# Moving the copy of the transposed V from ScalarE to VectorE in the attention stage of a transformer layer

## The reference, cut to what matters

```python
# layer: x = x + attn(layernorm(x)); x = x + ffn(layernorm(x))   x: 1 x 8192 x 2048, fp32
def attn(x, w_qkv, w_proj):                 # 16 heads of 128
    qkv = (x @ w_qkv.T).reshape(B, N, 3, H, hd)
    q, k, v = (qkv[:, :, 0], qkv[:, :, 1], qkv[:, :, 2])
    att = jnp.einsum('bnid,bnjd->bnij', q, k) * hd ** (-0.5)   # over the 16 heads of one row
    att = jax.nn.softmax(att, axis=-1)
    out = jnp.einsum('bnij,bnjd->bnid', att, v)
    out = out.transpose(0, 2, 1, 3).reshape(B, N, D)
    return out @ w_proj.T
def ffn(x, kernel, bias):                   # 8-bit fake quantisation of x, kernel, bias, y
    y = jax.nn.relu(fq(x, -1) @ fq(kernel, 0) + fq(bias, -1))
    return fq(y, -1)
```

## Time and profile before

| | us |
|---|---|
| Time, median of 2 runs | 911.78 (911.33 to 912.23) |
| The profiled execution: its own time | 915.79 |
| its span, slowest core (core 6) | 914.2 |
| spans of the 8 cores | 902.3 to 914.2 |
| VectorE busy | 553.4 (61%) |
| ScalarE busy | 336.6 (37%) |
| TensorE matmuls busy | 692.9 (76%) |

### The profile page before, as it was taken

One profiled execution on the slowest core, in us unless ns is written; L12 is line 12 of the kernel. 1 busy time (PEld: TensorE's weight loads), 2 busy tenths in 40 slices (PEclk: granted clock), 3 DMA queues, 4 the chain that ended last, 5 costly groups with the idle time before them and its releaser, 6 DMA issues.

```text
span 914.2 us, 11027 instructions; the slowest of 8 cores (902.3 to 914.2 us)
## 1 busy us (share of the span) xinstructions
PE 692.9 (76%) x3584; PEld 339.7 (37%) x3584; DVE 553.4 (61%) x917; ACT 336.6 (37%) x395; POOL 110.9 (12%) x93
## 2 busy tenths in 40 slices
PE   1158999899999999994555568974985756978891
PEld 1023444344444444443444434530332323433340
DVE  3352335345554554434555528993598896899997
ACT  3366334233433433435666622220121334333320
POOL 1000111111111111100000000002000000123214
PEclk9998999899999999996555568985798967999996
DMA  9462999899999999857522354459322200111112
GB/s 165 137 187 16 83 77 149 121 145 148 162 146 147 157 156 103 77 47 200 133 35 36 38 160 138 130 125 184 83 80 92 93 0 1 47 47 47 63 75 92
DMA packets 116983, 94.19 MB, mean 103 GB/s; under 512 B 101184, under 2 KB 101312, under 8 KB 113856
## 3 DMA queue, kind: packets, MB, share of 16 engines
q0 software_dynamic: 103680, 33.56, 38.5%
q1 hardware_dynamic: 13248, 59.94, 19.2%
HBM read 118.65 MB, written 8.39 MB: 139 GB/s over the span
## 4 chain that ended last, share of the span: by engine, by line
DVE 19%; PE 17%; issue 8%; DMA 5%; ACT 4%; DVEq 1%; POOLq 0%; POOL 0%; ACTq 0%; SPq 0%
DMA wpb<-wpT 4%; PE pF L535 3%; PE pF L499 3%; PE pF L502 3%; DVE bnbuf L588 2%; PE pF L343 2%; PE pH L334 2%; ACT aTTbuf L368 2%; ACT V8buf L362 2%; DVE ttile L796 2%; DVE cols L653 2%; PE pF L324 1%; PE pH L317 1%; DVE cols L799 1%; DVE ktb L685 1%
## 5 line engine op out<-in xcount | busy, mean ns | idle before, releaser
L286 PE MATMUL pF<-aT,wqb 128*128 128x512 bf16 x736 | 280.7, 381 | 5.8 <-DMA wqb<-wqkvT 5.8
L288 PE MATMUL pF<-aT,wqb 128*128 128x512 bf16 x736 | 280.5, 381 | 0.0
L499 PE MATMUL pF<-wpb,sT 128*128 128x512 bf16 x256 | 105.7, 413 | 24.2 <-DMA wpb<-wpT 22.1
L535 PE MATMUL pF<-qk,xqs 128*128 128x512 bf16 x512 | 118.8, 395 | 3.7 <-ACT xqs L882 3.7
L286 PEld LDWEIGHTS pF<-aT,wqb 128*128 128x128 bf16 x736 | 72.4, 98 | 95.1 <-issue 9.5
L502 PE MATMUL pF<-wpb,sT 128*128 128x512 bf16 x256 | 106.0, 414 | 0.0
L288 PEld LDWEIGHTS pF<-aT,wqb 128*128 128x128 bf16 x736 | 72.3, 98 | 87.3 <-issue 1.7
L301 POOL DMA_DIRECT2D wqb<-wqkvT x48 | 55.0, 1146 | 339.7 <-PE pF L288 250.9
L113 DVE CAST qT<-pF 128x512 bf16<-128x512 f32 x16 | 42.7, 2671 | 73.9 <-PE pF L288 59.3
L113 DVE CAST vT<-pF 128x512 bf16<-128x512 f32 x16 | 42.8, 2673 | 58.7 <-PE pF L288 58.7
L535 PEld LDWEIGHTS pF<-qk,xqs 128*128 128x128 bf16 x512 | 51.6, 102 | 67.7 <-issue 13.0
(11 more groups left out here) (116 smaller groups left out, 855.6 us busy)
## 6 DMA issues: line engine op xcount, KB each, us to landing
wqb<-wqkvT POOLq DMA_DIRECT2D x48, 512.0 KB, 10.0
ktc<-wkT SPq DMA_DIRECT2D x32, 512.0 KB, 8.3
ktb<-wkT SPq DMA_DIRECT2D x32, 512.0 KB, 3.8
xbuf<-x_att SPq DMA_DIRECT2D x8, 1024.0 KB, 6.3
xr<-x_res SPq DMA_DIRECT2D x8, 1024.0 KB, 7.5
wpb<-wpT POOLq DMA_DIRECT2D x32, 256.0 KB, 5.9
out<-xr SPq DMA_DIRECT2D x7, 1024.0 KB, 3.8
bias_b<-bias SPq DMA_DIRECT2D x1, 1024.0 KB, 4.6
```

Of the source, the lines that this page charges most:

```text
L286: tn.matmul(pa[:, :], wch, aT[:, 1024 * c:1024 * c + 512], start=st, stop=sp)
L288: mm = tn.matmul(pb[:, :], wch, aT[:, 1024 * c + 512:1024 * c + 1024], start=st, stop=sp)
L499: tn.matmul(pF[2 * (idx % 2)][:, :], lhs, wpb[:, 1024 * m:1024 * m + 512], start=st, stop=sp)
L535: mm = tn.matmul(pF[u][:, :], xqs[Mt % 2][:, 128 * c:128 * (c + 1)], qk[:, 2048 * c + 512 * u:2048 * c + 512 * (u + 1)], start=(c == 0), s ...
```

## The change

The 32 copies of the transposed V leave ScalarE's program and enter VectorE's, at the head of each turn, ahead of the wait for exp. They keep their two waits (cV8t, and cO8 from g = 2 on), and their operands and semaphore. `tensor_copy` takes the place of ScalarE's `copy`. Nothing else is edited.

```diff
@@ scalar
                     inc(s.activation(Ebuf[g % 2][:, :], pF[g % 2][:, :], AF.Exp,
                                      bias=col(80), scale=SCALE), "cExp")
-                    s.wait_ge(S_("cV8t"), g + 1)
-                    if g >= 2:
-                        s.wait_ge(S_("cO8"), g - 1)
-                    inc(s.copy(V8buf[g % 2][:, :], pH[2 + g % 2][:, :]), "cV8e")
+
@@ vector
             for g in range(NG + 1):
                 if g < NG:
                     p = g % 2
+                    v.wait_ge(S_("cV8t"), g + 1)
+                    if g >= 2:
+                        v.wait_ge(S_("cO8"), g - 1)
+                    inc(v.tensor_copy(V8buf[g % 2][:, :], pH[2 + g % 2][:, :]),
+                        "cV8e")
                     v.wait_ge(S_("cExp"), g + 1)
```

## The result

The changed kernel took 907.19 us (median of 12 runs, 905.43 the lowest) against 913.38 (11 runs) for the kernel before, measured beside it. The ratio is 0.991, with a 95% interval of 0.989 to 0.994. That is a gain of 0.9%, under the 2% at which it would be called faster. In the ratio it is 7.9 us, in the medians 6.2, where 7.5 was forecast, and 907.19 lies in the forecast range. The profiled execution of the changed kernel has a slowest span of 905.9 us on core 4.

What follows compares the result with a forecast made beforehand. ScalarE's order was taken as the bound at 3.60 us a round; 29 rounds saving 0.27 each give 7.8 us, less 0.3 for late starts, so 911.8 - 7.5 = 904.3 us, range 901 to 908.

Steps and rivals of the forecast that it cites:

- The removal: Attention stage, ScalarE: without the copy of V, the weights copy follows exp at 0.59 us, not 1.05, freeing 0.46 per group.
- ScalarE's round: Attention stage, exp through weights copy and line 343 to the next exp: 0.59 + 0.96 + 1.59 = 3.14 us per group.
- The loop that is late next: Exp, mask, scalings, line 334, weights copy, line 343, exp after next: 6.67 us for two groups, a round of 3.33.
- Rival (a): Attention stage: only ScalarE's round binds, as VectorE-to-TensorE hand-overs are shorter; 13.3 us gained, 898.5 us; chance 0.07.
- The copy on VectorE: VectorE, attention stage: 32 copies out of PSUM at 0.70 us each (0.4 to 2.68), hidden by its idle time.
- the threshold of 0.99: VectorE, attention stage: copies of V stop being hidden at 3.33 - 2.34 = 0.99 us per copy.
- The wait for the transposes of V: VectorE, head of each turn: the copy waits for line 317, ends some 0.2 us behind exp's start, and holds nothing up.
- Rival (d): VectorE's slow PSUM copy becomes the bound at line 383; over 1.26 us per copy costs time, up to 953; chance 0.06.
- The late starts: VectorE, attention stage: occasional late starts, no longer hidden, take 0.3 us off the 7.8 us saving, leaving 7.5.
- Start, end, hand-over: Around the attention stage: exp of group 2 stays at 425.88, the tail stays, and the ktb load hands the gain on whole.
- Rival (c): The gain is given back behind the stage, or the copy takes about 1.26 us; 912 us; chance 0.13.
- rival (b): TensorE's clock rises above 0.50 in the attention stage; 16 us gained, 895.5 us, or 892; chance 0.06.

## Why the prediction was right

**The removal.** The weights copy now follows exp at 0.58 (0.59 was said), and ScalarE's round is 3.11 (3.14 was said). The experiment without the mask shows it as the bound.

One reading of the chain was loose. From line 324 the view goes on through line 334 to the copy of V, and not to the exp:

```profile
472.68 0.54 PE pH L334 x4
```

Line 334 did not bind there. In the next round it ended at 476.31 + 0.58 = 476.89, and the weights copy that reads its result started only at 477.48, behind exp and the copy of V. The sum of the ScalarE round uses start times of the timeline and does not hang on this step.

**The loop that is late next.** This was the step on which the size hung, since ScalarE's round alone would have given 13.3 us. The loop's sum was 6.67 us for two groups, and undisturbed pairs show 3.11 + 3.54 = 6.65. Its terms come out one by one as well. In the pair above they are 0.78 from exp to the mask (0.79 was said), 2.45 to the end of the scalings (2.34, and the late one), 0.25 to line 334 (0.25), 0.73 to the weights copy (0.74), 0.94 to line 343 (0.96) and 1.60 to the exp (1.59). The alternation that was forecast is there. Adding 0.53 to the loop cost 0.27 a round, taking 0.53 out brought ScalarE's round back, and the same removal before the change did nothing. Rival (a) is out. One sentence of the forecast does not fit its own sum: of the 0.46 us a group that ScalarE gives free, a round of 3.33 in place of 3.14 takes 0.19, two fifths and not more than half. The sum used 3.33, so the number did not suffer.

**The copy on VectorE.** It was put at 0.70 from the fp32 reads in the earlier trace rows. It took 0.42, and 0.33 start to start. The size was off by 0.28 us a copy, outside the 0.6 to 0.75 that had been named as a sign of being right, and this did no harm to the forecast, because the threshold of 0.99 was far from both. The wait for the transposes of V held next to nothing up: in the waits of the changed kernel, 422 to 521 us, it stands with one case.

```profile
DVE Embuf L385 <- ACT Ebuf L357: 17.9, 29, 1.1
DVE V8buf L382 <- PE pH L317: 0.3, 1, 0.3
```

VectorE's idle time ahead of the mask fell from 36.7 us to 17.9 us, 0.62 a group. The forecast of some 0.3 was low by about the 0.28 by which the copy was priced too dear. Rival (d) needed copies of over 1.26 us.

**The late starts.** They were mis-sized. 29 rounds at 6.67 / 2 would take 96.7 us and took 97.3, so they cost 0.6 where 0.3 was taken off, and 0.8 if counted from the measured pair of 6.65. The rounds saved 7.2 us and not 7.5. The 0.3 rested on one gap in one group, so that it was out by no more than 0.5 us is luck.

**Start, end, hand-over.** From the first exp to that of group 2 nothing moved. The exp of group 2 itself stands at 423.44 and not at the 425.88 that was forecast, because that execution reached the stage 2.4 us sooner (first exp at 417.05 against 419.49). The change touches nothing ahead of the stage, so this is no part of its gain. From the last exp to the last sT it is 526.48 - 520.71 = 5.77 us against 536.36 - 530.38 = 5.98. The idle 0.35 us ahead of line 395 in the earlier trace rows did not recur (scalings follow the reciprocal by 0.10 elsewhere, so they were 0.25 late there and not 0.35). The gain was not given back. From the last sT to the end it took 377.8 to 382.2 us on the eight cores before, 379.3 in the mean, and 377.6 to 381.1 after, 379.5 in the mean. The whole kernel gained 7.9 us by the ratio, the stage 7.2 + 0.2. Rival (c) is out.

**The clock.** It stood at 0.50 with matmuls busy 58.16 of 97.20 us, 60%, so rival (b) did not occur.

## What to carry to other kernels

When an operation leaves the engine whose order is the bound, first sum the next loop, counted over as many groups as it spans: it sets how much of the removed time comes back (here 0.25 of 0.46 us a group). An operation's cost is decided by whether it lies inside the binding loop. A second copy of 0.33 us in VectorE's idle time was free, a second mask of 0.53 us in the loop cost the whole gain, and with a deeper pipeline that fills VectorE the move itself costs 0.3 us a group. Here, where all engines were partly idle in a steady alternation, another group in flight was worth more than moving work (4.4% against 0.9%).

## What was not expected of the hardware

A copy of a 128x512 bf16 PSUM tile takes VectorE 0.42 us, where the two operations that read a PSUM tile of that shape in fp32, a TENSOR_TENSOR and a TENSOR_SCALAR, take 0.68 to 0.74 and ScalarE takes 0.58 for the bf16 copy. By the Trainium skill (VectorE: DVE Perf Modes, The TRN2 errata) I had estimated 0.66 us at one element per cycle and 0.39 at two. The measured 0.42 is near the estimate at two. Which of the type and the operation makes the difference to the fp32 rows, no run here separates.

TensorE's clock behaved differently in the two deeper pipelines. Their windows from the exp of group 2 to that of group 31, columns as in the earlier trace rows, first with the copy on ScalarE:

```profile
425.50:491.97 66.47, 46.59 (x463) 35.61 (x461) 56.94 (x203) 62.59 (x117) 7.41 (x14) 0.75 0.58 133
```

and with the copy on VectorE:

```profile
422.80:498.24 75.44, 58.53 (x463) 44.47 (x461) 65.97 (x233) 51.10 (x89) 7.41 (x14) 0.50 0.52 117
```

The first had a mean granted clock of 0.75, moving between 1.2 and 2.4 GHz: line 350 took 0.38 us at 455.97 and 0.58 at 458.31. The second stayed at 1.2 GHz with matmuls busy 78% of the time, more than the first's 70%. The two shares are not of a kind, since matmuls are shorter at the higher level. Two stretches of the first, four turns of VectorE each from mask to mask, show it:

```profile
440.08:449.65 9.57, 8.00 (x67) 6.19 (x64) 7.94 (x28) 8.82 (x17) 1.06 (x2) 0.50 0.75 200
467.87:476.88 9.01, 4.89 (x64) 3.71 (x64) 7.76 (x29) 8.46 (x17) 1.06 (x2) 1.00 0.43 68
```

At 1.2 GHz matmuls were busy 84% of the time, at 2.4 GHz 54%. What lets the clock rise in the one kernel and not in the other was not tried and stays open.

The round of the first depended little on the clock. At 2.4 GHz a turn took 9.01 / 4 = 2.25 us. At 1.2 GHz the turns were 2.26, 2.35, 2.61 and 2.35, the longest with 0.46 us of idle time ahead of VectorE's sums, where it is 0.1 elsewhere. Whether the clock has a part in these 0.1 us was not tried. Between the two deeper kernels the rounds differ by 0.31 us, 9.0 us in 29, and the ratios by 7.7 us of 919. From the last sT to the end they took 381.3 and 381.6 us, so the difference lies in the stage, and the copy's 0.34 us a turn is enough for it.
